# A vision block on one core: the first attention's residual added on TensorE through the identity, and copied out of PSUM by ScalarE

## The chip, the core and the metric

The kernel runs on one core of one Trainium2 chip. The metric is the device time of one execution in microseconds (us). The engines are TensorE (PE; PEld is its weight load), VectorE (DVE), ScalarE (ACT), GpSimd (POOL) and SyncE (SP, which here only starts DMAs). They run side by side and are ordered by semaphores alone.

## The reference, cut to what matters

```python
h = tok(x)                                            # (16, 37, 256)
h = h + attn(layernorm(h), Wqkv, Wout, bout)          # <- this sum is what the change moves
h = h + ffn(layernorm(h), w_q, w_k, w_gate, value_experts, output_experts)

def layernorm(x): return (x - mean(x)) / sqrt(var(x) + 1e-5)
def attn(x, Wqkv, Wout, bout):                        # 16 heads of 16
    ...                                               # rotary numerator, plain denominator, causal
    return y @ Wout + bout
```

Everything is float32. There are 16 images of 37 tokens, 592 tokens in all, of width 256.

## The kernel before, in words

Tokens stand on the partitions in six groups of three images: group g holds R = 111 tokens (the sixth one image and padding), and `h[:, g]` is its 111x256 slice of the residual stream. `h` is filled by the embedding; POOL adds the bias of the output projection to it early (line 460, semaphore `h0b_ready`). The first attention works in NB = 4 batches of four images: scores (L1228), exponentials on ScalarE (L644), the causal mask on VectorE (L910), attend (L1246), denominators (L1258), their reciprocal `rden` on VectorE (L927) and the product `yT` (L932), which is the attention's output with the width on the partitions.

Each engine runs its own instruction list in order; all lists are written out by hand. The stretch that the change touches is this:

- TensorE, inside the last batch: `out_proj(0)`, `out_proj(1)`, the denominators of the last batch, `out_proj(2)`, `out_proj(3)`, then `attend` of the last batch in two halves with `turn_x2(0)` (L1285) between them. Groups 0 to 3 need only the first three batches (`yT_ready` 3), groups 4 and 5 need the last. `D_ORDER` gives what follows: turn 1, turn 2, gate 0, qk 0, out 4, out 5, qk 1, turn 3, qk 2, qk 3, turn 4 and so on. qk jobs are the projections of the second attention (L263 to L265: three reduced-precision passes for one float32 product).
- VectorE: `residual(g)` waits until both groups of a pair are projected (`op_ps` counts to `g // 2 * 2 + 2`), adds PSUM to `h[:, g]` (L947) and takes the layer norm's statistics (`ln_stats`: L803, L804, L805). `ln_apply` (L814) makes `xhat` once POOL has taken the power in L447. `turn_x2` transposes `xhat` and `h` into PSUM, ScalarE copies them out as `h1T` (L668) and `x2hi` (L669), and `x2_lo` (L954) takes the rest. The list is: residual 0, residual 1, apply 0, residual 2, apply 1, x2_lo 0, apply 2, x2_lo 1, x2_lo 2, then the reciprocal and product of the last batch, then residual 3 and so on.
- ScalarE between the last exponentials and the evacuation of turn 0 has nothing.

`out_proj(g)` for one group is two matmuls in float32 over the two halves of the width; each shows as two rows in the trace (two passes), so a pair of groups shows as x8.

The final stage multiplies expert outputs under masks (`gx`, L1095) and accumulates on TensorE.

Of the kernel before, what the change touches and what calls it, by code (L numbers as in the profile page):

```python
# [9 lines left out]
ACT = mybir.ActivationFunctionType  # L10
# [11 lines left out]
D = 256  # L22
KC = D // P
# [4 lines left out]
G = -(-B // GI)  # L28
R = GI * S
# [79 lines left out]
def vit_block(nc, x, tokw, vecs, consts, wqkv, wout, w2, ve, oe, mask_rows, out):  # L109
    with ExitStack() as ctx:  # L110
        def sem(name):
            return ctx.enter_context(nc.semaphore(name))

        def sbuf(stack, name, shape, dt=F32, side="left"):
            return stack.enter_context(nc.sbuf_tensor(name, shape, dt, side=side))


        cst = sbuf(ctx, "cst", [P, NCONST])
# [4 lines left out]
        h = sbuf(ctx, "h", [R, G, D])  # L123
# [110 lines left out]
        ps = ctx.enter_context(nc.psum_tensor("ps", [P, 8, 512], F32))  # L234
# [17 lines left out]
        sm = {n: sem(n) for n in names}  # L252
# [44 lines left out]
        NOP = (NB - 1) * BI * S // R  # L297
        OPB = [(4 + g // 2, g % 2 * D) if g < NOP else (1, (g - NOP) * D) for g in range(G)]
# [222 lines left out]
        def _(act):  # L521
# [108 lines left out]
            def exps(b, kind):  # L630

                if kind == 0 and b >= 2:
                    act.wait_ge(sm["pv_ps"], b - 1)
                if kind == 1 and b >= 1:
                    act.wait_ge(sm["den_ps"], b)
                for t in range(2):
                    act.wait_ge(sm["s_ps"], 4 * b + 2 * kind + t + 1)
                    src = ps[0:2 * S, 2 * t:2 * t + 2, 0:KC * 2 * JS * S]
                    if kind == 0:
                        dst = en[:, b % 2, t].rearrange("p r c i j s -> p r (c i j s)")  # L640
                    else:
                        src = src.rearrange("p r (c x) -> p r c x", c=KC)
                        dst = ed[:, :, :, 2 * t:2 * t + 2].rearrange("p r c i j s -> p r c (i j s)")
                    act.activation(dst, src, ACT.Exp, scale=DH1 ** -0.5).then_inc(sm["exp_ready"], 1)  # L644
# [8 lines left out]
            def ve_hi(e):  # L653
                act.wait_ge(ve_in[e % NVR], 16 * (e // NVR + 1))
                if e >= NVR:
                    act.wait_ge(sm["ve_ps"], NT * (e - NVR + 1))
                act.activation(vehi[:, e % NVR], veraw[:, e % NVR], ACT.Copy).then_inc(sm["vehi_ready"], 1)  # L657

            for b in range(NB):
                exps(b, 0)  # L660
                exps(b, 1)
                if b < NVR:
                    ve_hi(b)
            def x2_hi(g):

                act.wait_ge(sm["x2T_ps"], g + 1)
                src = ps[:, 2 + g % 2, 0:2 * KC * R].rearrange("p (a c t) -> p a c t", a=2, c=KC)
                act.activation(h1T[:, :, g * R:(g + 1) * R], src[:, 1], ACT.Copy)  # L668
                act.activation(x2hi[:, :, g * R:(g + 1) * R], src[:, 0], ACT.Copy).then_inc(sm["x2hi_ready"], 1)  # L669

            def exp_gate(t):
                act.wait_ge(sm["gate_ps"], t + 1)
                act.activation(ez[0:TROWS[t], t], ps[0:TROWS[t], t % 2, 0:NH2 * NE], ACT.Exp,
                               scale=-1.0).then_inc(sm["ez_ready"], 1)

            def qk2_evac(n):
                hf, c, kind = QK2[n]
                act.wait_ge(sm["qk2_ps"], n + 1)
                src, col = ps[:, 4 + n % 4, 0:HALF], slice(hf * HALF, (hf + 1) * HALF)
                if kind == "k":  # L680
                    act.activation(k2[:, c, col], src, ACT.Copy).then_inc(sm["qk2_ready"], 1)
                else:
                    for p_ in range(2):
                        ins = act.activation(q2[:, c, 8 * hf:8 * hf + 8, p_], src.rearrange("p (i s) -> p i s", s=S),
                                             ACT.Copy, scale=cols("par")[:, 2 + p_:3 + p_])
                    ins.then_inc(sm["qk2_ready"], 1)

            for kind, n in D_ORDER:
                if kind == "turn":
                    x2_hi(n)  # L690
                elif kind == "gate":
                    exp_gate(n)
                elif kind == "qk":
                    qk2_evac(n)
# [68 lines left out]
        def _(dve):  # L763
            count = {}

            def step(name, ins):

                count[name] = count.get(name, 0) + 1
                ins.then_inc(sm[name], 1)
                dve.wait_ge(sm[name], count[name])  # L770
# [31 lines left out]
            def ln_stats(which, g):  # L802
                step("lnchain", dve.bn_stats(stat6[:, which], h[:, g]))  # L803
                step("lnchain", dve.bn_aggr(mv[:, which, g], stat6[:, which]))  # L804
                dve.tensor_scalar(lnv[:, which, g:g + 1], mv[:, which, g, 1:2], 1e-5, None,  # L805
                                  ALU.add).then_inc(sm["lnv_ready"], 1)
# [135 lines left out]
            causal(NB - 1)  # L942

            def residual(g):
                dve.wait_ge(sm["op_ps"], g // 2 * 2 + 2)
                dve.wait_ge(sm["h0b_ready"], g + 1)
                step("h1_ready", dve.tensor_tensor(  # L947
                    h[:, g], h[:, g], ps[0:R, OPB[g][0], OPB[g][1]:OPB[g][1] + D], ALU.add))
                ln_stats(1, g)

            def x2_lo(g):
# [4 lines left out]


            residual(0)
            residual(1)
            ln_apply(1, 0)  # L960
            residual(2)
            ln_apply(1, 1)
            x2_lo(0)
# [111 lines left out]
            for k in range(1, C2 * NE):  # L1075
                c, w = k // NE, k // MEU
                if k % NE == PV_AT + 3 and c + 1 < C2:

                    o = PVB[c + 1]
# [26 lines left out]
        def _(pe):  # L1106
# [155 lines left out]
            def out_proj(g):  # L1262
                if g < NOP:
                    pe.wait_ge(wout_in, 16)
                    pe.wait_ge(sm["yT_ready"], NB - 1)
                else:
                    pe.wait_ge(sm["yT_pad"], 1)
                    pe.wait_ge(sm["yT_ready"], NB)
                o, w = OPB[g]
                for k in range(KC):  # L1270
                    ins = pe.matmul(ps[0:R, o, w:w + D], yT[:, k, g * R:(g + 1) * R], wo[:, k],  # L1271
                                    start=(k == 0), stop=(k == KC - 1))
                ins.then_inc(sm["op_ps"], 1)

            def turn_x2(g):
# [12 lines left out]
            for b in range(NB):  # L1288
                scores(b, 0)
                if b:  # L1290
                    denominators(b - 1)
                scores(b, 1)
                if b == NB - 1:
                    out_proj(0)
                    out_proj(1)
                    denominators(b)
                    for g in range(2, NOP):
                        out_proj(g)
                attend(b)
# [251 lines left out]
```

## Time and profile before

| | us |
|---|---|
| median of 3 runs | 249.35 (249.26 to 249.85) |
| the profiled execution | 248.44 |
| its span | 246.6 |
| TensorE busy | 216.5 |
| VectorE busy | 175.3 |
| ScalarE busy | 102.2 |
| GpSimd busy | 76.3 |

Times in the rows are us from the start of the span of the one profiled execution. Busy time counts instructions that overlap once. A group of rows in a timeline is merged: `x8` is eight instructions that ran one behind the other. An entry in brackets is how long the engine was idle before and who ended it. L12 is line 12 of the kernel.

### The profile page before, as it was taken

The page shows a single profiled execution, that of the slowest core. Times are in us where ns is not written, and L with a number is a line of the kernel's source. Part 1 is how long each engine was busy: PE and PEld are TensorE (multiplying, and loading weights), DVE is VectorE, ACT ScalarE, POOL GpSimd, SP SyncE. Part 2 cuts the span into 40 slices and gives each one's busy share as a digit, 9 for nine tenths or more (in the row PEclk, how much of TensorE's full clock was granted, in tenths as well). Part 3 has the DMA queues.
Part 4 walks back from the last instruction along what each step waited for, and adds up shares of the span by engine and source line. Part 5 has one row for each costly group of instructions (what it writes and reads, how often), then busy time and mean ns, then how long its engine had stood idle before and what let it go on. Part 6 is the DMA issues. An engine that isn't in the chain of part 4 may idle for free.

```text
span 246.6 us, 5111 instructions
## 1 busy us (share of the span) xinstructions
PE 216.5 (88%) x2047; PEld 190.7 (77%) x2047; DVE 175.3 (71%) x321; ACT 102.2 (41%) x202; POOL 76.3 (31%) x79
## 2 busy tenths in 40 slices
PE   0155879999787899999999999999999999999993
PEld 0035669999674579997768888877989989999993
DVE  1779888654898766942436575666699979979972
ACT  3777859856753216575432161554301111020000
POOL 1152787000342241300506538565934000000000
PEclk9999999999999959999999999999999999999999
DMA  6998000000000020000422005109305154431102
GB/s 177 261 326 352 1 3 1 3 0 0 5 3 3 3 85 1 3 0 0 162 110 85 3 1 185 72 13 254 103 0 169 66 186 142 167 110 49 52 0 100
DMA packets 7181, 20.08 MB, mean 81 GB/s; under 512 B 1043, under 2 KB 1878, under 8 KB 6902
## 3 DMA queue, kind: packets, MB, share of 16 engines
q1 hardware_dynamic: 7158, 19.76, 25.3%
q8 instruction: 16, 0.26, 0.4%
q14 instruction: 7, 0.06, 0.1%
HBM read 19.07 MB, written 0.68 MB: 80 GB/s over the span
## 4 chain that ended last, share of the span: by engine, by line
PE 60%; DVE 27%; issue 6%; ACT 2%; DMA 1%; POOL 1%; DVEq 0%; POOLq 0%
PE ps L263 16%; PE ps L264 15%; PE ps L265 15%; DVE gx L1095 7%; PE ps L1396 3%; DVE rden L927 2%; PE ps L1271 2%; PE ps L1426 2%; DVE oelo L1069 2%; DVE en L910 2%; PE ps L1228 2%; DVE amax L774 1%; DMA xp<-x_rows 1%; DVE stat L803 1%; DVE xhat L814 1%
## 5 line engine op out<-in xcount | busy, mean ns | idle before, releaser
L1033 DVE COPY_PREDICATED v<-onehot,ps 128x512 f32<-128x512 uint8 (+3 forms) x40 | 26.2, 660 | 24.1 <-PE ps L265 23.9
L1095 DVE TENSOR_TENSOR gx<-maskb,oT 128x1184 fp32r<-128x1184 bf16 x31 | 42.3, 1411 | 0.6 <-PE ps L265 0.5
L263 PE MATMUL ps<-gx,oelo 128*128 128x296 f32 x124 | 37.8, 305 | 0.6 <-DVE gx L1095 0.6
L265 PE MATMUL ps<-gx,oehi 128*128 128x296 f32 x124 | 37.2, 300 | 0.0
L264 PE MATMUL ps<-gx,oehi 128*128 128x296 f32 x124 | 37.0, 298 | 0.0
L263 PE MATMUL ps<-vehi,x2lo 128*128 128x512 f32 (+3 forms) x90 | 35.1, 390 | 0.0
L264 PE MATMUL ps<-velo,x2hi 128*128 128x512 f32 (+3 forms) x90 | 33.3, 370 | 0.0
L265 PE MATMUL ps<-vehi,x2hi 128*128 128x512 f32 (+3 forms) x90 | 33.1, 368 | 0.0
L470 POOL TENSOR_TENSOR velo<-veraw,vehi 128x1024 fp32r<-128x1024 f32 x8 | 19.1, 2392 | 23.4 <-ACT vehi L657 18.4
L263 PEld LDWEIGHTS ps<-gx,oelo 128*128 128x128 f32 x124 | 23.3, 188 | 1.8 <-issue 1.3
L264 PEld LDWEIGHTS ps<-gx,oehi 128*128 128x128 f32 x124 | 23.4, 189 | 0.0
L265 PEld LDWEIGHTS ps<-gx,oehi 128*128 128x128 f32 x124 | 23.3, 188 | 0.0
L263 PEld LDWEIGHTS ps<-vehi,x2lo 128*128 128x128 f32 (+1 forms) x90 | 16.2, 180 | 3.9 <-issue 0.7
L1131 PE MATMUL ps<-ident_bf,qb 111*128 111x111 bf16 x36 | 4.5, 297 | 16.8 <-DVE qb L799 16.7
L265 PEld LDWEIGHTS ps<-vehi,x2hi 128*128 128x128 f32 (+1 forms) x90 | 16.2, 180 | 3.7
L264 PEld LDWEIGHTS ps<-velo,x2hi 128*128 128x128 f32 (+1 forms) x90 | 16.3, 181 | 2.8
L1131 PEld LDWEIGHTS ps<-ident_bf,qb 111*128 111x128 bf16 x36 | 3.1, 138 | 18.7 <-DVE qb L799 18.6
L728 ACT ACTIVATE oehi<-oeraw 128x1024 fp32r<-128x1024 f32 x8 | 8.5, 1059 | 18.7 <-DMA oeraw<-output_w 18.7
L442 POOL TENSOR_TENSOR w2lo<-w2raw,w2hi 128x544 fp32r<-128x544 f32 x4 | 6.3, 1590 | 28.5 <-PE ps L1258 28.5
L707 ACT ACTIVATE pe<-sc 74x444 f32<-74x444 f32 (+1 forms) x6 | 3.2, 533 | 24.1 <-POOL sc L485 24.1
L447 POOL TENSOR_TENSOR rstd<-lnv,half_neg 111x1 f32<-111x1 f32 x12 | 7.9, 657 | 16.6 <-DVE lnv L805 16.6
L263 PE MATMUL ps<-x2hi,w2lo 128*128 128x296 f32 x32 | 11.0, 345 | 0.0
(159 smaller groups left out, 521.9 us busy)
## 6 DMA issues: line engine op xcount, KB each, us to landing
maskb<-mask_rows SPq DMA_DIRECT2D x32, 148.0 KB, 3.6
veraw<-value_w SPq DMA_DIRECT2D x8, 512.0 KB, 3.7
oeraw<-output_w SPq DMA_DIRECT2D x8, 512.0 KB, 3.7
xp<-x_rows SPq DMA_DIRECT2D x6, 336.0 KB, 9.1
wqraw<-w_qkv SPq DMA_DIRECT2D x1, 1280.0 KB, 13.0
w2raw<-w_qkgate SPq DMA_DIRECT2D x1, 1088.0 KB, 15.0
tw<-tok_weight SPq DMA_DIRECT2D x1, 768.0 KB, 7.8
out<-yo SPq DMA_DIRECT2D x4, 148.0 KB, 1.9
```

Source lines behind the costliest of these rows:

```text
L263: pe.matmul(o, llo, rhi, start=start, stop=False)
L264: pe.matmul(o, lhi, rlo, start=False, stop=False)
L265: return pe.matmul(o, lhi, rhi, start=False, stop=stop)
L442: pool.tensor_tensor(w2lo[:, n // 2, part], w2raw[:, n // 2, part], w2hi[:, n // 2, part].bitcast(F32), ALU.subtract).then_inc(sm["w2lo_re ...
L447: pool.tensor_tensor(rstd[:, which, g:g + 1], lnv[:, which, g:g + 1], half_neg[0:R, 0:1], ALU.pow).then_inc(sm["rstd_ready"], 1)
L470: pool.tensor_tensor(velo[:, e % NVR], veraw[:, e % NVR], vehi[:, e % NVR].bitcast(F32), ALU.subtract).then_inc(sm["velo_ready"], 1)
L728: act.activation(oehi[u % NOR][:], oeraw[RAW[u]][:], ACT.Copy).then_inc(sm["oehi_ready"], 1)
L910: dve.tensor_tensor(v, v, bcast(cols("keep", 2 * S), 1, 2 * KC * JP), ALU.mult).then_inc(sm["en_ready"], 1)
L1033: dve.copy_predicated(v2[0:m, t, h0:h1], bcast(onehot[0:m, t, h0:h1, e], 2, DH2), ps[0:m, JBANK[n], 0:(h1 - h0) * DH2].rearrange("p (a b) ...
L1095: dve.tensor_tensor(gx[:, k % NGR].rearrange("p a b t -> p a (b t)"), bcast(maskb[:, w % NMR, k % MEU], 1, 2), oT[:, c % 2].bitcast(F32), ...
L1131: ins = pe.transpose(dst[:, c * (R + 1):c * (R + 1) + R], qb[:, g % NQB, c * P:(c + 1) * P], ident_bf[0:R, 0:R])
L1396: ins = pe.matmul(ps[0:2 * S, 2 + g % 2, u * S:(u + 1) * S], q2[:, c, i].rearrange("p a b -> p (a b)"), k2[:, c, tc], start=True, stop=True)
```

## The change

TensorE starts each output projection with a third matmul, the 111x111 identity against `h[:, g]`, into the same PSUM columns, and accumulates the two old ones onto it. ScalarE copies the finished sum from PSUM to `h[:, g]` (`residual_out`): groups 0 to 3 ahead of everything in `D_ORDER`, groups 4 and 5 between qk 0 and qk 1. VectorE's `residual(g)` no longer adds: it waits for ScalarE's copy and takes the statistics.

```diff
@@ scalar
+            def residual_out(g):
+
+                act.wait_ge(sm["op_ps"], g // 2 * 2 + 2)
+                act.activation(h[:, g], ps[0:R, OPB[g][0], OPB[g][1]:OPB[g][1] + D], ACT.Copy).then_inc(sm["h1_ready"], 1)
+
...
+            for g in range(NOP):
+                residual_out(g)
             for kind, n in D_ORDER:
                 if kind == "turn":
                     x2_hi(n)
+                elif kind == "out":
+                    if n == G - 1:
+                        for g in range(NOP, G):
+                            residual_out(g)
@@ vector
             def residual(g):
-                dve.wait_ge(sm["op_ps"], g // 2 * 2 + 2)
-                dve.wait_ge(sm["h0b_ready"], g + 1)
-                step("h1_ready", dve.tensor_tensor(
-                    h[:, g], h[:, g], ps[0:R, OPB[g][0], OPB[g][1]:OPB[g][1] + D], ALU.add))
+                dve.wait_ge(sm["h1_ready"], g + 1)
                 ln_stats(1, g)
@@ tensor, out_proj(g), behind its waits for yT
                 o, w = OPB[g]
+                pe.wait_ge(sm["h0b_ready"], g + 1)
+                pe.matmul(ps[0:R, o, w:w + D], cst[0:R, 0:R], h[:, g], start=True, stop=False)
                 for k in range(KC):
                     ins = pe.matmul(ps[0:R, o, w:w + D], yT[:, k, g * R:(g + 1) * R], wo[:, k],
-                                    start=(k == 0), stop=(k == KC - 1))
+                                    start=False, stop=(k == KC - 1))
                 ins.then_inc(sm["op_ps"], 1)
```

## Rows read from the trace of the kernel before

**Rows 1.** The page: busy time of the engines, and the chain's shares.
```profile
PE 216.5 (88%) x2047; PEld 190.7 (77%) x2047; DVE 175.3 (71%) x321; ACT 102.2 (41%) x202; POOL 76.3 (31%) x79
...
PE 60%; DVE 27%; issue 6%; ACT 2%; DMA 1%; POOL 1%; DVEq 0%; POOLq 0%
```

**Rows 2.** Busy time by stretch, all engines; the first and last of nine stretches.
```profile
core 0: us, PE busy (x) PEld busy (x) DVE busy (x) ACT busy (x) POOL busy (x), PEclk, DMA share, GB/s
93.00:103.00 10.00, 10.00 (x80) 9.86 (x80) 8.04 (x23) 6.72 (x20) 3.60 (x3) 0.99 0.01 2
...
173.00:183.00 10.00, 10.00 (x123) 9.61 (x122) 7.39 (x19) 2.24 (x4) 6.03 (x8) 1.00 0.17 54
```

**Rows 3.** The chain that ended last, 77 to 93 us: start, length, what.
```profile
77.81 1.97 PE ps L1271 x8
...
79.79 0.43 DVE h L947
...
83.89 0.66 POOL rstd L447
...
85.04 0.61 PE ps L1285 x4
...
86.62 2.01 DVE rden L927
...
88.66 0.48 DVE yT L932
...
89.27 3.72 PE ps L1271 x8
```

**Rows 4.** Timeline of TensorE, 77 to 93 us: start, length, work.
```profile
79.69 0.72 PE L1258 MATMUL ps<-ed,cst 74*32 74x296 f32 x8
80.34 1.98 PE L1271 MATMUL ps<-wo,yT 128*111 128x256 f32 x8
82.25 0.48 PE L1246 MATMUL ps<-en,vblk 74*32 74x37 f32 x32
```

**Rows 5.** Timeline of VectorE, 81 to 87 us.
```profile
82.14 0.15 DVE L805 TENSOR_SCALAR lnv<-mv 111x1 f32<-111x1 f32 x1
...
82.53 0.41 DVE L947 TENSOR_TENSOR h<-h,ps 111x256 f32<-111x256 f32 x1
82.98 0.43 DVE L803 BATCH_NORM_STATS2 stat<-h 111x6 f32<-111x256 f32 x1
...
83.66 0.15 DVE L805 TENSOR_SCALAR lnv<-mv 111x1 f32<-111x1 f32 x1
...
84.57 0.41 DVE L814 TENSOR_SCALAR xhat<-h,mv,rstd 111x256 f32<-111x256 f32 x1
...
86.32 0.39 DVE L954 TENSOR_TENSOR x2lo<-ps,x2hi 128x222 fp32r<-128x222 f32 x1 [0.45 <-ACT x2hi L669]
```

**Rows 6.** Timeline of ScalarE, 73 to 106 us: copies out of PSUM.
```profile
85.68 0.36 ACT L668 ACTIVATE h1T<-ps 128x222 f32<-128x222 f32 x1 [0.23 <-PE ps L1285]
...
88.71 0.42 ACT L681 ACTIVATE k<-ps 128x296 f32<-128x296 f32 x1 [1.47 <-PE ps L265]
94.04 0.91 ACT L684 ACTIVATE q<-ps,cst 128x296 f32<-128x296 f32 x2 [4.91 <-PE ps L265]
```

**Rows 7.** Busy time of TensorE and its clock, as a share of full speed.
```profile
core 0: us, PE busy (x), PEclk, DMA share, GB/s
78.00:84.00 6.00, 5.70 (x92) 1.00 0.01 3
84.00:86.40 2.40, 1.65 (x13) 1.00 0.00 0
86.40:89.20 2.80, 2.27 (x10) 0.51 0.00 0
89.20:93.20 4.00, 3.93 (x10) 0.50 0.38 131
93.20:96.00 2.80, 2.80 (x23) 0.99 0.01 3
```

**Rows 8.** Timeline of VectorE, 93 to 96 us.
```profile
93.03 0.42 DVE L947 TENSOR_TENSOR h<-h,ps 111x256 f32<-111x256 f32 x1 [1.64 <-PE ps L1271]
...
95.47 0.41 DVE L814 TENSOR_SCALAR xhat<-h,mv,rstd 111x256 f32<-111x256 f32 x1
```

## The prediction

> **What bounds the kernel now.** I read the page first, for which engine is busy and whose work the last-ended chain is made of. TensorE is busy 216.5 of 246.6 us and holds 60% of the chain, VectorE 27% [rows 1]. That is an average, so the second view is the busy time by stretch: from 93 to 183 us TensorE is busy in the whole of each of the nine stretches of 10 us, with 1.00 of its clock but for the first [rows 2]. It has no idle time there that could take up a delay, so whatever moves the moment at which this dense part begins moves the end by as much. The later part, 183 us on, follows from it and alternates between TensorE and VectorE, with no piece that is tied to an absolute time.
>
> The third view is the chain of waits just ahead of the dense part, where the change lies. There the chain goes through the first pair of output projections (77.81 us, x8), VectorE's adds and statistics, POOL's power (83.89), the last batch's reciprocal (86.62, 2.01 us), its product (88.66), and the second use of L1271, groups 4 and 5, at 89.27 us [rows 3]. Behind these TensorE is dense. So the price of the change is read from this stretch of 15 us: when does the reciprocal start, and how long do groups 4 and 5 take after it.
>
> The fourth view is TensorE's clock. It is at its upper level, 2.4 GHz, while TensorE is busy 5.70 of 6.00 us; then come 2.4 us in which it is busy 1.65 with narrow work and transposes, and the granted clock falls to 0.50 (1.2 GHz) at about 86.4 and is back at about 93.3, after four nearly full microseconds [rows 7]. The same eight passes of L1271 take 1.97 us at the upper level and 3.72 at the lower [rows 3].
>
> **The change, step by step.**
>
> *More TensorE work.* One more float32 matmul of 256 columns for each group, two passes. A pass of an old one costs (1.98 us less the overlap at its end) / 8: the pair starts at 80.34 and the next work at 82.25, so 1.91 / 8 = 0.24 us [rows 4]. At the lower clock it is 3.72 / 8 = 0.465 [rows 3]. The new one has the same 256 streamed columns and a weight block of 111x111 instead of 128x111. The trace has no such matmul, and I bound it: above by the old pass; below by the transposes with the same identity, four of 111 columns in 0.61 us [rows 3], 0.15 each, if a pass did not care for its columns. I take 0.24, since the columns and their number are the old pass's own; at 0.15 the sum below would be about 1.05 less. Four extra passes for each pair: 0.96 us at 2.4 GHz, 1.86 at 1.2. The first pair and the second each grow by 0.96, with the denominators (0.65 us from 79.69 to 80.34) between them unchanged, so the second pair ends at 82.32 + 2 x 0.96 = 84.24. The wait for `h0b_ready` costs nothing: POOL filled `h` long before this stretch. The identity stands behind the wait for `yT`, so nothing hides it.
>
> *A hop through ScalarE in place of the add.* Removed: six adds on VectorE of 0.41 to 0.43 us [rows 3, 5]. Added: six copies of 111x256. The trace has copies out of PSUM of 222 columns (0.36 us) and 296 (0.42) [rows 6]; in between, 256 gives about 0.39, bounds 0.36 and 0.42. An engine starts about 0.02 to 0.04 us after its releaser. So a copy plus a hop replaces an add at nearly the same latency, and VectorE's own load is lighter. For the first two groups: copies end at about 81.1 and 81.4, statistics of group 1 end at about 82.8, against 82.29 before (82.14 + 0.15 [rows 5]): half a microsecond late, of no weight by itself.
>
> *Where it bites: group 2.* Before, VectorE came to residual 2 at 82.53 [rows 5], just after the second pair was done (82.32), and never waited. Now the pair ends at 84.24, ScalarE's copy at 84.24 + 0.02 + 0.39 = 84.65, and VectorE, which does its list in order, stands still from about 83.1 until 84.69. Queued behind this wait are apply 1, x2_lo 0, apply 2, x2_lo 1, x2_lo 2 and the reciprocal of the last batch; TensorE's turn 1, turn 2 and gate 0 wait for them in turn, and ScalarE's copies for those. From the start of the statistics to their end is 83.66 + 0.15 - 82.98 = 0.83 us; so 85.52. POOL starts 0.08 later (83.81 to 83.89) and takes 0.66 [rows 3, 5], so 86.26, and `xhat` of group 2 starts at 86.28 instead of 84.57: 1.71 later. From there turn 2, ScalarE's two copies and x2_lo 2 take 86.32 - 84.57 = 1.75 as before (88.03), and the reciprocal starts 0.30 behind it, at 88.33 instead of 86.62. The other legs come earlier: turn 1 can start when `xhat` 1 is done, 85.43 + 0.41 = 85.84, and is over before turn 2 at 86.7. The reciprocal could have run before, since its denominators are ready by 81.4; the order of the list puts it last. Groups 4 and 5 then start at 89.27 + 1.71 = 90.98.
>
> *Groups 4 and 5.* Twelve passes for eight. At one level of the clock throughout, they add 0.96 or 1.86. Behind the pair, VectorE gains: without the second add, `xhat` 4, which before started 2.44 us behind the pair's end (93.03 to 95.47 [rows 8]), comes about 0.5 earlier. It gives nothing back, since TensorE had no idle time there [rows 2]. ScalarE's two copies of about 0.28 us spacing stand ahead of the evacuation of qk 1, which before started at 94.04, 1 us behind the pair [rows 6]: covered.
>
> *The clock.* Before, 89.27 to 93.28 ran at half rate, which cost 4.0 / 2 = 2.0 us on the path; the part before 89.27 cost nothing, the reciprocal being what TensorE waited for. After, the thin stretch is there again: attend's halves from 84.2 to 85.7, then turns, gate 0, qk 0, and idle time to 90.98, over five microseconds of little work, as before. So I expect the fall again. If TensorE stays low for the same 4.0 us after the pair's start, the loss is the same 2.0 and the sum is 1.71 + 0.96 = +2.67. If it stays low through all twelve passes (5.58 us), the pair ends at 96.56 for 92.99: +3.57. If it does not fall, the 2.0 come back: +0.67.
>
> *The sum.* The profiled execution took 248.44 (span 246.6 and 1.8 around it), 0.91 less than the median of the runs shown, 249.35, which I put down to how long the low clock lasted in it. I take +2.67, the case in which the low time is as before, and apply it to the median: 252.0 us. Against the profiled execution it gives 251.1, and with the upper bound of the clock 252.0.
>
> **The rivals.**
>
> *The clock stays up.* For it: the TensorE stretch ahead of the fall is now longer and denser (12 + 12 passes from 77.8 to 84.2). Against it: the thin stretch behind it is still as long as the one that brought the fall in [rows 7]. Time: 249.35 + 0.67 = 250.0. The Trainium skill ("TensorE: Matmul & The Clock Gate", Part 1) says that the lower rate is the resting state and that activity releases it; by that rule more matmul work works in this rival's favour, and rows 7 agree in direction (low after thin work, up after dense).
>
> *Faster: VectorE's list is the path, and the identity passes hide under it.* Before, VectorE ran from 79.79 to 84.98 without a wait, and three adds of 0.43 stand in it ahead of the reciprocal. If TensorE were ready in time, the first add's place would be taken by the copy and the other two would vanish: -0.86, 248.5. It decides at the moment group 2's copy must be there, about 83.0 us: with 82.32 + 0.41 for pair and copy, eight extra passes may take 0.3 us together, 0.035 each. The nearest row says 0.24. The Trainium skill ("VectorE: DVE Perf Modes", Rules for kernel authors) advises to lower the count of VectorE's operations in a chain, which speaks for the change; the row that stands against it is L1271's.
>
> *The low clock lasts longer.* The fall comes later and the whole of groups 4 and 5 and some of qk 1 run at half rate: +3.6 or a little more, 252.9 to 253.4.
>
> *Absorbed.* The dense part has a hidden wait on something that isn't late. Rows 2 speak against it in all nine stretches. About 249.5.
>
> **How the numbers follow.** Forecast (+1.6 to +3.3 us, low clock about as long as before): 0.66. Longer low clock (+3.3 to +4.2): 0.12. Clock stays up (+0.2 to +1.2): 0.12; half of it is within 0.3% (0.75 us), about what a measurement of this kernel can tell from no change, and half slower. Absorbed: 0.05. Faster rival: 0.05. So faster 0.05, same 0.11, slower 0.84. The range reaches from the rival at 250.0, less its spread of 0.3 (249.7), to 253.4, the long low clock's end; what is left out is the faster rival, the absorbed case and the far end of the longest, under 0.15 together. The forecast's own range is 250.9 (identity passes at their lower bound) to 252.7.
>
> **What would show it.** In the changed kernel's profile: (1) L1271 and the identity at x12 a pair, 2.9 us for each of the first two; any shorter, and the first step is wrong. (2) VectorE idle 1.5 us ahead of the statistics of group 2, ended by ScalarE's copy. (3) The reciprocal of the last batch at 88.3. (4) Groups 4 and 5 from 91.0 and a granted clock of 0.5 in them. (5) TensorE busy without a gap from there for 90 us. (6) Copies of 0.39 us. The prediction is wrong if (3) fails, because then the delay was taken up elsewhere, or if (4) shows the clock at 1.00.

## The result, and the profile after

| | before | changed |
|---|---|---|
| median, 7 runs each | 249.35 us (248.55 to 249.95) | 251.40 us (250.41 to 252.65) |
| profiled execution: span | 246.6 us | 249.0 us |
| TensorE busy | 216.5 us | 217.0 us |
| VectorE busy | 175.3 us | 173.3 us |

The ratio is 1.0087, with a 95% interval of 1.0056 to 1.0119: 2.2 us slower (1.4 to 3.0). All ratios below are to the kernel before, run beside the kernel on the same chip. They leave out executions more than 1.5% above the fastest of their kernel: 2 of 11, 3 of 12 and 1 of 12 of the kernels with VectorE's copy, with the passes only and with the first fillers, and 1 of 6, 5 of 9 and 3 of 11 of those with the reciprocal's move, whose ratios therefore leave out most or all of a slower course that is shown below.

The profiled execution of the changed kernel (250.75 us, mean clock 0.991) is not a typical one: five of the seven had a mean clock of 0.986 and took 251.4 to 252.65 us. So the low clock lasted longer in most executions than in the profile shown here, and the account in microseconds below is that of the two profiled executions.

The times in a span start from different moments: the first pair of output projections starts at 77.81 us before and at 78.23 in the changed kernel, though nothing ahead of it was changed, and between 77.2 and 78.7 in the experiments. In four of the experiments' profiles the low clock came a second time, far ahead of the change, at about 33 to 36 us, and their first pair starts at 78.27 to 78.39; the changed kernel's profile has no low clock there, so the cause of its 0.42 us is open. I measure every kernel from the start of its first pair. TensorE in the changed kernel (timeline: start, length, work; L1279 is the identity, L1281 the old matmuls) answers to [rows 3, 4]:

```profile
78.23 0.66 PE L1279 MATMUL ps<-h,cst 111*111 111x256 f32 x2 [1.52 <-issue]
78.72 1.03 PE L1281 MATMUL ps<-wo,yT 128*111 128x256 f32 x4
...
80.98 0.72 PE L1266 MATMUL ps<-ed,cst 74*32 74x296 f32 x8
81.63 0.69 PE L1279 MATMUL ps<-h,cst 111*111 111x256 f32 x2
...
84.41 0.48 PE L1254 MATMUL ps<-en,vblk 74*32 74x37 f32 x32
...
91.18 1.17 PE L1279 MATMUL ps<-h,cst 111*111 111x256 f32 x2 [1.31 <-issue]
92.13 1.91 PE L1281 MATMUL ps<-wo,yT 128*111 128x256 f32 x4
93.84 0.94 PE L1279 MATMUL ps<-h,cst 111*111 111x256 f32 x2
94.62 1.03 PE L1281 MATMUL ps<-wo,yT 128*111 128x256 f32 x4
95.30 0.48 PE L263 MATMUL ps<-x2hi,w2lo 128*128 128x296 f32 x1
```

A pair is twelve passes: 78.23 to 80.98 is 2.75 us, 0.23 a pass. The pair of groups 4 and 5 starts 12.95 us behind the first pair (11.46 before), and in it the same work takes 4.12 us, its first identity 1.17 for 0.66: the clock is low.

VectorE in the changed kernel answers to [rows 5]:

```profile
81.50 0.43 DVE L814 BATCH_NORM_STATS2 stat<-h 111x6 f32<-111x256 f32 x1 [2.01 <-ACT h L667]
...
84.93 0.43 DVE L814 BATCH_NORM_STATS2 stat<-h 111x6 f32<-111x256 f32 x1 [1.52 <-ACT h L667]
...
86.53 0.41 DVE L825 TENSOR_SCALAR xhat<-h,mv,rstd 111x256 f32<-111x256 f32 x1
...
88.27 0.39 DVE L962 TENSOR_TENSOR x2lo<-ps,x2hi 128x222 fp32r<-128x222 f32 x1 [0.45 <-ACT x2hi L674]
88.58 2.00 DVE L938 RECIPROCAL rden<-ps 128x296 f32<-128x296 f32 x1
```

The bracket in the second row is the new wait: 1.52 us ahead of group 2's statistics, ended by ScalarE's copy. From there to the reciprocal nothing has changed in kind (1.74 us from `xhat` to `x2lo`, 1.75 before). The reciprocal starts 10.35 us behind the first pair, for 8.81.

TensorE's clock in the changed kernel, by stretch (busy time, then the granted clock), answers to [rows 7]:

```profile
87.50:91.00 3.50, 2.01 (x14) 1.00 0.00 0
91.00:94.40 3.40, 3.22 (x8) 0.52 0.41 154
94.40:98.00 3.60, 3.60 (x26) 0.98 0.00 0
```

The clock fell again, but 3.4 us long instead of 6.8, and almost wholly in groups 4 and 5. Behind qk 1 TensorE is dense as before (10.00 of 10.00 us in each stretch from 93 to 183). The span is then a sum of three parts:

| | start of first pair | first pair to qk 1 | qk 1 to the end |
|---|---|---|---|
| before | 77.81 | 14.62 | 154.19 |
| changed | 78.23 | 17.07 | 153.66 |

Of the 0.53 us less behind qk 1, 0.3 is the clock again, which before was still low there (the kernel before with a steady clock, below, has 153.88).

### The profile page after: what moved, and what is told of

Its sections match the earlier page's. It is cut to its first block, busy times and chain, and to the rows that moved or that the text cites. A ratio compares the mean times of both kernels' runs of the same rounds, so it can differ in the third digit from the quotient of the medians.

```text
span 249.0 us, 5129 instructions
## 1 busy us (share of the span) xinstructions
PE 217.0 (87%) x2059; PEld 190.9 (77%) x2059; DVE 173.3 (70%) x315; ACT 104.1 (42%) x208; POOL 76.2 (31%) x79
## 4 chain that ended last, share of the span: by engine, by line
PE 63%; DVE 24%; issue 7%; DMA 3%; ACT 1%; SPq 0%; DVEq 0%
PE ps L263 16%; PE ps L264 15%; PE ps L265 15%; DVE gx L1103 7%; DMA tw<-tok_weight 3%; PE ps L1406 3%; PE ps L1281 2%; PE ps L1436 2%; PE ps L1236 2%; DVE oelo L1077 2%; DVE en L921 2%; PE ps L1279 2%; DVE amax L785 1%; PE ps L1295 1%; DVE stat L814 1%
## 5 line engine op out<-in xcount | busy, mean ns | idle before, releaser
L263 PE MATMUL ps<-x2hi,w2lo 128*128 128x296 f32 x32 | 10.3, 323 | 0.1
```

Of the source, the lines that this page charges most:

```text
L263: pe.matmul(o, llo, rhi, start=start, stop=False)
```

## The experiments

**Who pays: the hop or the passes.** Three kernels take the change apart. The kernel before, run beside them, had a median of 248.82 us. In the first VectorE copies the sum itself, and ScalarE's copies are gone (VectorE's list shown):

```diff
-                dve.wait_ge(sm["h1_ready"], g + 1)
+                dve.wait_ge(sm["op_ps"], g // 2 * 2 + 2)
+                step("h1_ready", dve.tensor_copy(h[:, g], ps[0:R, OPB[g][0], OPB[g][1]:OPB[g][1] + D]))
                 ln_stats(1, g)
```

> The changed kernel, but VectorE copies the sum out of PSUM (and waits for TensorE itself) instead of ScalarE. My theory: the price lies in TensorE's extra passes, which make the second pair of projections late, and the copy's engine is nothing to it. Then the last batch's reciprocal starts as long behind the first pair's start as in the changed kernel (88.58 - 78.23 = 10.35 us, give or take 0.1), and the median stays at 251.4, within 0.5. The rival, that the hop through ScalarE costs: the distance falls towards 8.8 us (before) and the median by up to 1.5, to 249.9.

Measured: 10.39 us from the first pair to the reciprocal, median 251.54, ratio 1.0065 (1.0025 to 1.0105). As my theory has it: which engine copies changes the distance by 0.04 us, and the two ratios (1.0065 and 1.0087) lie within each other's intervals.

In the second the identity goes and ScalarE's copy stays; the first old matmul starts the sum again:

```diff
-                pe.wait_ge(sm["h0b_ready"], g + 1)
-                pe.matmul(ps[0:R, o, w:w + D], cst[0:R, 0:R], h[:, g], start=True, stop=False)
...
-                                    start=False, stop=(k == KC - 1))
+                                    start=(k == 0), stop=(k == KC - 1))
```

> The changed kernel without the identity matmul, so that the residual is left out of the first attention's sum and ScalarE copies the bare projection: the hop alone. My theory: the reciprocal starts 8.6 us behind the first pair, 0.2 less than before (8.81), since the second pair's end (4.51 us behind the first's start) and not the removed add sets when the statistics of group 2 can start; the median is 249.1, no change from before (0.996 to 1.003). The prediction's faster rival (VectorE's list is the path, three adds vanish) gives 7.95 us and 248.5. The rival that the hop costs gives 9.3 us or more and 249.9 or more.

Measured: 8.61 us to the reciprocal, median 248.35, ratio 0.9964 (0.9939 to 0.9990). The distance is the forecast one, 0.20 less than before, and far from the faster rival's 7.95. VectorE's timeline in this kernel shows why:

```profile
80.67 0.43 DVE L815 BATCH_NORM_STATS2 stat<-h 111x6 f32<-111x256 f32 x1 [1.19 <-ACT h L668]
...
83.24 0.43 DVE L815 BATCH_NORM_STATS2 stat<-h 111x6 f32<-111x256 f32 x1 [0.66 <-ACT h L668]
```

Even with eight passes a pair, VectorE stands 0.66 us ahead of group 2: it lost its adds and found the second pair not there yet. The median fell by more than these 0.2 us (by 0.47, to the edge of what I had given), while in its profiled execution the first pair to qk 1 takes 14.42 for 14.62. The mean clocks say where the rest may come from: five of its twelve executions had 0.992 or 0.993, of the 34 of the kernel before beside it only four, and where the mean clock was 0.986 in both, the mean times were 248.69 and 248.61 us.

In the third the kernel before gets the passes and nothing else; the next matmul overwrites them:

```diff
+                pe.wait_ge(sm["h0b_ready"], g + 1)
+                pe.matmul(ps[0:R, o, w:w + D], cst[0:R, 0:R], h[:, g], start=True, stop=True)
                 for k in range(KC):
```

> The kernel before, with VectorE's add, and with the identity matmul issued ahead of the two old ones, which overwrite it: the passes alone. My theory: the whole price is here, reciprocal 10.35 us behind the first pair's start, twelve passes for groups 4 and 5, median 251.4 within 0.5. The rival, that the hop has a share: less than 251.0 and a distance below 10.

Measured: 10.39 us, median 251.54, ratio 1.0080 (1.0043 to 1.0117). VectorE, which still adds, waits at the same place:

```profile
85.00 0.42 DVE L947 TENSOR_TENSOR h<-h,ps 111x256 f32<-111x256 f32 x1 [0.61 <-PE ps L1273]
...
89.10 2.00 DVE L927 RECIPROCAL rden<-ps 128x296 f32<-128x296 f32 x1
```

The passes alone bring the whole price, as far as the intervals tell (1.0080 and 1.0087, each within about 0.4%). In this kernel's profiled execution, 252.13 us and one of its three longest, the low clock lasted from about 89.6 to 96.4: groups 4 and 5 took 4.77 us for 4.12, and the first pair to qk 1 17.76 for 17.07. How long the clock stays low thus adds or takes 0.7 us for the same work.

**Groups 4 and 5: the identity ahead of the wait.** The two identity matmuls are taken out of `out_proj(4)` and `out_proj(5)` and issued earlier:

```diff
+                    if n == NOP:
+                        pe.wait_ge(sm["ez_ready"], 1)
+                        for g in range(NOP, G):
+                            seed(g)          # the identity matmul of g, group 5 in bank 0
                     out_proj(n)
```

> The changed kernel, with the identity matmuls of groups 4 and 5 moved ahead of the wait for the last batch's product, into TensorE's idle time of 1.3 us (group 5 in a bank of its own). My theory: the pair behind the wait is back at eight passes, so 0.87 us less at 2.4 GHz and up to 1.5 at 1.2: median 250.0 to 250.5; the reciprocal's distance stays 10.35. If the clock stays up because TensorE is busier there, another 1.6 less: 248.9. If groups 4 and 5 were not on the path: no change.

Measured: 10.34 us to the reciprocal, ratio 0.9991 (0.9961 to 1.0020), 2.4 us less than the changed kernel. TensorE's timeline:

```profile
88.70 1.03 PE L1273 MATMUL ps<-h,cst 111*111 111x256 f32 x4
90.21 1.95 PE L1286 MATMUL ps<-wo,yT 128*111 128x256 f32 x8 [0.47 <-DVE yT L943]
91.81 0.48 PE L263 MATMUL ps<-x2hi,w2lo 128*128 128x296 f32 x1
```

The identities run while TensorE would have waited, the pair is back at eight passes, and the clock is at 1.00 all the way. The first pair to qk 1 takes 14.59 us for 17.07. The move is worth about 0.8 of it (14.59 against the 15.41 of the changed kernel at a steady clock, below); the rest is the clock. This profile is the fastest of the kernel's twelve executions. Five had a mean clock of 1.000 and took 247.4 to 248.2 us; seven had 0.990 to 0.993 and took 249.0 to 249.9, and so the median, 249.19, lies between my two forecasts.

**The clock.** First, fillers in the idle time just ahead of groups 4 and 5:

```diff
+                    if n == NOP:
+                        pe.wait_ge(sm["h1_ready"], NOP)
+                        filler(3)            # pe.matmul(ps[:, 5, 0:D], cst[:, 0:P], wo[:, 0]), unused
                     out_proj(n)
```

> The changed kernel with three more matmuls (six passes, 1.3 us) in TensorE's idle time between qk 0 and groups 4 and 5, into a bank that is free; their result is not used. My theory of the clock: it falls in the thin stretch ahead of groups 4 and 5, and work there keeps it up. Then the trace has no low clock in 80 to 100 us, the distance from the first pair to qk 1 is 15.5 us for 17.07 in the changed kernel, and the ratio to before is 1.002 to 1.004 for 1.0087. If the clock had no part in the time, or falls all the same: 17.07 and 1.009. If the filler itself is late: 17.3 or more.

Measured: 16.79 us, ratio 1.0055 (1.0030 to 1.0081). I had expected 15.5. Clock and timeline of this kernel:

```profile
84.80:88.20 3.40, 2.52 (x48) 1.00 0.02 5
88.20:91.60 3.40, 3.33 (x11) 0.52 0.00 0
```

```profile
89.96 2.35 PE L1314 MATMUL ps<-wo,cst 128*128 128x256 f32 x6
92.14 0.60 PE L1279 MATMUL ps<-h,cst 111*111 111x256 f32 x2
```

In this execution the clock fell at 88.3, before the fillers began. They ran at half rate, took 2.35 us for 1.4, and were late themselves: the last pair starts at 14.37 us for 12.95. So in this execution the idle time just ahead of the pair did not bring the clock down, and the work there came too late. It isn't so in all of them: five of the twelve had a mean clock of 0.996 to 1.000 and took 248.5 to 249.7 us, the other seven 0.992 or 0.993 and 250.0 to 252.8, while the changed kernel's seven all had 0.991 or less. The next two kernels fill every gap of the thin stretch, the changed kernel's (shown) and the earlier one's alike (there 6, 3, 3 and 8):

```diff
+            def filler(n):
+                for _ in range(n):
+                    pe.matmul(ps[:, 1, 0:P], ident_bf[:], ident_bf[:], start=True, stop=True)
...
+                        filler({1: 5, 2: 3}.get(n, 0))
                         turn_x2(n)
                 elif kind == "gate":
+                    filler(3 if n == 0 else 0)
                     gate_job(n)
                 elif kind == "out":
+                    filler(16 if n == NOP else 0)
```

> The changed kernel with small bf16 matmuls (128 columns, result unused, in the bank that groups 4 and 5 overwrite) in each idle gap of TensorE's thin stretch: 5 ahead of turn 1, 3 ahead of turn 2, 3 ahead of gate 0, 16 ahead of groups 4 and 5. If thin work there brings the clock down, the clock stays at 1.00 from 80 to 100 us, the first pair to qk 1 takes 15.7 us for 17.07, and the ratio to before is 1.003 for 1.0087. If the fall has another cause: 17.1 and 1.009.

> The kernel before with the same fillers (6, 3, 3 and 8). If thin work brings the clock down: no low clock, the first pair to qk 1 takes 13.3 us for 14.62, ratio 0.993. Together with the changed kernel filled it gives the price of the change with the clock taken out of it: 1.49 + 0.87 = 2.4 us, or 1.0095 between the two ratios. If the clock were the main part of the price, the two would lie within 0.3%.

Measured: changed and filled 15.41 us, ratio 1.0029 (1.0003 to 1.0056); before and filled 13.06 us, ratio 0.9921 (0.9896 to 0.9946). Both ratios as forecast, the distances 0.2 to 0.3 us shorter. The clock by stretch, of the changed kernel filled and then of the one before filled:

```profile
84.00:86.40 2.40, 2.31 (x62) 1.00 0.02 7
86.40:91.00 4.60, 4.01 (x38) 1.00 0.00 0
91.00:95.00 4.00, 4.00 (x27) 1.00 0.37 131
```

```profile
84.00:86.40 2.40, 2.22 (x20) 1.00 0.00 0
86.40:91.00 4.60, 3.61 (x26) 1.00 0.22 71
```

In the kernel before, TensorE was busy 1.65 us of the first stretch [rows 7], and the clock fell at its end; with small useless work in the gaps (2.22 us) it stays. The changed kernel had 2.01 of 3.50 us ahead of its fall; filled, it has 4.01 of 4.60 in the second stretch, and no fall. The executions without a trace agree: the 24 of these two kernels all had a mean clock of 0.991 or more, the 91 of the kernel before that ran beside the experiments all 0.993 or less. So the fillers keep the clock up. That thin work always brings it down is not shown: the kernel with the early identities had 1.81 of 2.40 us in 84.0 to 86.4 and no fall, the kernel of the next section 1.80 in the same stretch and a fall at 87.4, and that same kernel went without a fall in other executions.

Two things follow. In these executions the fall costs both kernels about as much, 17.07 - 15.41 = 1.7 us here and 14.62 - 13.06 = 1.6 us there (and 0.3 behind qk 1); with the longer low clock of the kernel with the passes only it is 17.76 - 15.41 = 2.35. And with the clock out of it, the change costs 15.41 - 13.06 = 2.35 us up to qk 1, or 1.1% between the two ratios.

**The reciprocal.** The last theory to test is that the delay goes through VectorE's list. The last batch's denominators go ahead of the first pair on TensorE and its reciprocal ahead of residual 0 on VectorE, where the changed kernel idles 2.0 us:

```diff
                 if b == NB - 1:
+                    denominators(b)
                     out_proj(0)
                     out_proj(1)
-                    denominators(b)
...
+            denominators(NB - 1)
             residual(0)
...
             x2_lo(2)
-            denominators(NB - 1)
             normalise(NB - 1)
```

> The changed kernel, with the last batch's denominators ahead of the first pair on TensorE (idle there) and its reciprocal ahead of residual 0 on VectorE (2.0 us idle there). My theory, that the delay goes through VectorE's in-order list to the reciprocal: group 2's statistics 6.0 us behind the first pair's start (6.70), groups 4 and 5 at 10.7 (12.95), so 2.2 us less, ratio 1.000; if the shorter thin stretch also keeps the clock up, 0.994. If the reciprocal was not on the path: 1.009.

> The changed kernel with the reciprocal's move once more, since the profile shown of it lies far above its median (250.2 for 246.6) and has the low clock through groups 4 and 5. I expect a ratio of 0.990 to 0.995 again, and a profile near 246.6 in which the clock does not fall or falls for a shorter time, the first pair to qk 1 in 14 to 15 us for 16.09.

Measured: ratio 0.9916 (0.9891 to 0.9941) and 0.9931 (0.9882 to 0.9980). VectorE's timeline of the first:

```profile
79.55 2.00 DVE L938 RECIPROCAL rden<-ps 128x296 f32<-128x296 f32 x1
81.64 0.43 DVE L814 BATCH_NORM_STATS2 stat<-h 111x6 f32<-111x256 f32 x1
...
84.24 0.43 DVE L814 BATCH_NORM_STATS2 stat<-h 111x6 f32<-111x256 f32 x1 [0.69 <-ACT h L667]
...
87.57 0.39 DVE L962 TENSOR_TENSOR x2lo<-ps,x2hi 128x222 fp32r<-128x222 f32 x1 [0.45 <-ACT x2hi L674]
87.88 0.46 DVE L943 TENSOR_TENSOR yT<-ps,rden 128x296 f32<-128x296 f32 x1
```

The reciprocal fits exactly into the wait for the first copy, and the product follows x2_lo 2 at once. Group 2's statistics come at 5.87 us (6.0 expected, 6.70 in the changed kernel). But in both profiled executions the clock fell:

```profile
87.40:94.20 6.80, 6.80 (x23) 0.51 0.24 77
94.20:96.00 1.80, 1.80 (x14) 0.97 0.00 0
```

It was low for 6.8 us with TensorE busy in all of them, and the first pair to qk 1 took 16.09 us in each. Groups 4 and 5 start at 11.50 and 11.59 us for 10.7 expected; the two kernels with the move whose clock stays up (below) have 10.64 and 10.65. My expectation for the second, a profile near 246.6, failed. The other executions say that this is one of two courses: over both runs eight of fifteen took 246.0 to 247.1 us at a mean clock of 0.997 to 1.000, six took 249.8 to 251.1 at 0.978 to 0.985, and one lies between (249.0). Over all nine executions of the second run the median is 249.77 us, for 249.12 of the kernel before beside it: the move alone is not dependably faster.

The program is the same; the courses lie 3.5 to 4 us apart. The fall in this stretch makes about 3.0 of it (16.09 for the 13.04 and 13.06 of the kernels below). Both profiled executions also had the low clock earlier, where nothing was changed:

```profile
32.80:36.20 3.40, 3.40 (x15) 0.51 0.02 5
```

Their first pair starts at 78.37 and 78.33 us, for 77.51 and 77.48 in the two kernels below, which have no low clock there: another 0.85 us, which this fall would explain, though no run shows it by itself.

The same move in the kernel before, with the same edits:

> The same move in the kernel before, where VectorE has only 0.8 us idle at that place, so the reciprocal pushes its list back by 1.3 us. Groups 4 and 5 at 11.2 us behind the first pair (11.46), ratio 0.998 to 1.000, 0.993 if the clock stays up. Beside e6 it tells whether the change is worth more once the reciprocal is out of the way: by my numbers no, the passes still cost 0.87 in groups 4 and 5.

Measured: ratio 0.9995 (0.9977 to 1.0013). Groups 4 and 5 start at 12.45 us, for 11.2 expected, since the clock fell at about 85 and qk 0 ran at half rate right up to them. The move alone gives this kernel nothing as the clock was: all twelve executions had a mean clock of 0.979 to 0.986. What it gives at a steady clock is not shown.

The changed kernel with the move and the early identities, and with the move and the fillers ahead of turn 1, turn 2 and gate 0:

> The changed kernel with the reciprocal's move and with the identity matmuls of groups 4 and 5 ahead of their wait. They no longer have idle time to lie in if qk 0 ends later than the product comes, so I expect between nothing and 0.9 us less than the reciprocal's move alone: ratio 0.996 to 1.000 with a fall of the clock, 0.990 to 0.994 without.

> The changed kernel with the reciprocal's move and the fillers ahead of turn 1, turn 2 and gate 0. If the clock falls in part of the executions without fillers, this is faster than the move alone in the median and closer together: ratio 0.988 to 0.991 and a spread under 1.5 us. If not: the same as the move alone.

Measured: ratio 0.9928 (0.9902 to 0.9954) and 0.9928 (0.9898 to 0.9958); the first pair to qk 1 takes 13.04 and 13.06 us. The early identities add nothing here, as TensorE has no wait left to put them in:

```profile
88.00 0.30 PE L265 MATMUL ps<-x2hi,w2hi 128*128 128x296 f32 x1
88.13 0.60 PE L1279 MATMUL ps<-h,cst 111*111 111x256 f32 x2
...
90.54 0.49 PE L263 MATMUL ps<-x2hi,w2lo 128*128 128x296 f32 x1
```

These rows are of the move with the fillers: qk 0 runs into the last pair without a gap, at full clock. All nine of its executions took 245.9 to 248.0 us (median 247.34), where the move alone, run beside it, spread to 251.1 (median 249.77). Its expectation (0.988 to 0.991, a spread under 1.5 us) was a little too good, its direction right. With the early identities in place of the fillers three of eleven executions still took 250.2 to 250.9 us.

So the versions that beat both kernels dependably are the one before with fillers, and the changed one with the reciprocal's move and fillers: 0.9921 and 0.9928, no difference that the intervals can tell.

## Why the prediction was right, step by step

I forecast 252.0 us against a median of 249.35; measured were 251.4 and a ratio that gives 250.7 to 252.3. The sum was +2.67, the medians differ by 2.05. The path was the forecast one; the sizes of the passes and of the clock's part were a little too large, and the clock's part is in some measure luck, since it differs from one execution to the next.

- *Passes.* 0.24 us a pass taken, 0.23 measured; four extra cost 0.87 a pair for 0.96. My first sign read 2.9 us for a pair, "any shorter, and the first step is wrong"; it was 2.75. By that wording the sign failed, but it is the size of a pass that was 5% too large, with the twelve passes as forecast. That the bound of 0.15 from the transposes didn't hold is seen in the identity's own rows: as long as the old passes.
- *The hop.* Forecast 0.39 us for the copy, measured 0.381 (median of six). That it costs nothing that these runs can tell was shown by letting VectorE copy (10.39 us to the reciprocal for 10.35). The Trainium skill ("ScalarE: Activation LUTs", What ACT_TABLE_LOAD costs) gives 186 ns and 0.833 a column for such a copy, by which I estimate 0.399; the trace is 5% below.
- *Group 2.* The wait came where forecast, with 1.52 us for 1.6. The statistics of group 2 moved from 5.17 to 6.70 us behind the first pair, the reciprocal by 1.54 (it starts at 88.58; less the late start of the first pair, 88.16 for the 88.33 forecast), the start of groups 4 and 5 by 1.49, for 1.71 forecast. The difference is the pass: two pairs, each 0.09 too dear, are 0.18.
- *Groups 4 and 5.* 0.96 forecast for their four passes with the clock as before; 4.12 - 3.16 = 0.96 measured, by an accident of the clock. At full clock it is 0.86 (15.41 - 13.06, less the 1.49 by which the pair starts later, from the two filled kernels).
- *The clock.* I expected the fall again, with 4.0 us of low time behind the pair's start. It fell just as the pair began, at about 91.1, and was back at about 94.5, 3.3 us behind. Against the filled kernels the fall cost 17.07 - 15.41 = 1.66 us in the changed kernel and 1.56 + 0.31 = 1.87 in the one before (0.31 behind qk 1), for 2.0 in both forecast. The profiled executions then differ by 1.49 + 0.96 - 0.53 = 1.92 us, and 0.42 more from the late start of the first pair makes 2.34, the difference of the spans. Of the 0.75 that my 2.67 had too much against 1.92, the passes account for 0.32 (0.22 at the start of the pair, 0.10 in it), the clock for 0.21, and 0.2 lie behind qk 1, where the filled kernels too differ (153.88 and 153.67); for that I have no cause.
- *TensorE without a gap behind qk 1.* So it was; `xhat` 4 came 1.93 us behind the pair's end (95.67 to 97.60), for 2.44 before, and gave nothing back.
- *The rivals.* The clock's staying up came in none of the changed kernel's seven executions, but it was a real case: in the two kernels with the same matmuls (VectorE's copy, and the passes only) three of 23 executions had a mean clock of 0.998 or 0.999 and took 248.3 to 249.6 us, with the early identities five of twelve had 1.000. The Trainium skill ("TensorE: Matmul & The Clock Gate", Part 1) says that activity releases the low rate. The traces agree in direction, since the low stretch ended under the dense pair at about 94.5; that the same program keeps the clock in one execution and loses it in the next was in neither my argument nor these rows. The longer low clock was a real case as well: the kernel with the passes only shows it in its profile (17.76 us). The faster rival was mispriced, at 0.86: without any identity the reciprocal gains only 0.20, because the second pair becomes the next wait.

## What to carry to other kernels

Work moved onto an engine counts from the moment at which its result was needed, not by that engine's share of busy time: TensorE's 0.87 us of passes per pair sat right ahead of a list on VectorE that had 0.2 us of slack, while the add that they replaced was worth 0.2 us. Before an add is traded for passes, look for the idle time in which the passes can lie (here ahead of the wait for the product) and for what the receiver's new idle time can hold (here the reciprocal). And where a thin stretch on TensorE lies ahead of dense work on the path, look at the granted clock first: its fall cost about 1.6 us in the profiled executions of both kernels, more than half of what the change did. Look at it in several executions, too: a single profile shows one course of several.

## What the runs showed of the hardware that I had not expected

The clock's fall decides between courses of one and the same program: with the reciprocal's move, executions took 246.0 to 247.1 us or 249.8 to 251.1, at mean clocks of 0.997 to 1.000 or 0.978 to 0.985; in the two profiles of the slower course it fell twice, at 33 and at 87 us. Twenty-seven matmuls of 128 columns in bf16, whose results nobody reads, took the fall out of the changed kernel's profiled execution and 0.6% off its time. And work set just ahead of the dense part made little better where the fall had come before it (16.79 us for 17.07): at half rate the six passes took 2.35 us and were on the path themselves.
